# The gate of a two-layer image kernel: paired row strips, two engines that copy the turned magnitudes, a median step on VectorE alone, and attention maxima turned one product earlier

## What is computed

```
layer 0, for each image and channel:
    x = x + relu(-median(x))
    y = relu(up-sample x by 2 with a 7-tap filter); x = down-sample y by 2 with it
layer 1, for each image:
    spec = rfft2(x)
    gate = sigmoid(w2 . gelu(w1 . |spec|))          over the channels of each frequency
    xf   = x + irfft2(spec * gate)
    q    = xf . q_w + q_b                           16384 queries, 4 heads of 16
    k, v = from two strided convolutions of xf (256 and 64 places), layer norm, projection
    out  = softmax(q . k) . v, projected, plus x
```

## Time and profile before

| | us |
|---|---|
| runs | 11229.0, 11243.0, 11243.7 |
| median | 11243.0 |
| the profiled execution | 11240.2 |
| its span, first to last instruction | 11238.7 |
| busy in it: TensorE | 10118.1 (90%) |
| VectorE | 8624.4 (77%) |
| ScalarE | 7246.8 (64%) |
| GpSimd | 5892.8 (52%) |

### The profile page before, as it was taken

One profiled execution on the slowest core, in us unless ns is written; L12 is line 12 of the kernel. 1 busy time (PEld: TensorE's weight loads), 2 busy tenths in 40 slices (PEclk: granted clock), 3 DMA queues, 4 the chain that ended last, 5 costly groups with the idle time before them and its releaser, 6 DMA issues. The chain is left out here.

```text
span 11238.7 us, 198959 instructions
## 1 busy us (share of the span) xinstructions
PE 10118.1 (90%) x68889; PEld 4971.5 (44%) x69001; DVE 8624.4 (77%) x14560; ACT 7246.8 (64%) x12221; POOL 5892.8 (52%) x10577
## 2 busy tenths in 40 slices
PE   2898998989989899899989989899898998989989
PEld 1534435344353543535345353443534435354353
DVE  7777777877778777778777777777787777777777
ACT  5757566665666656667666676656666666675665
POOL 2374463735537365472744737446373553736547
PEclk9999999999999999999999999999999999999999
DMA  2031231312314032140322303123131331403214
GB/s 67 21 78 47 58 85 32 77 36 64 79 32 88 26 73 70 39 89 35 71 54 49 94 22 78 45 59 84 32 79 34 67 76 32 88 32 70 66 40 102
DMA packets 330611, 664.69 MB, mean 59 GB/s; under 512 B 95624, under 2 KB 241160, under 8 KB 308048
## 3 DMA queue, kind: packets, MB, share of 16 engines
q1 hardware_dynamic: 329552, 651.29, 24.4%
HBM read 232.53 MB, written 71.30 MB: 27 GB/s over the span
## 5 line engine op out<-in xcount | busy, mean ns | idle before, releaser
L1314 ACT ACTIVATE R<-ps 128x512 f32<-128x512 f32 x5120 | 2874.7, 593 | 1432.3 <-PE ps L807 1034.8
L1095 DVE TENSOR_REDUCE R<-ps 128x2 f32<-128x640 f32 x3840 | 3042.7, 819 | 798.0 <-PE ps L786 748.7
L265 ACT ACTIVATE R<-R,st 128x1475 bf16<-128x1475 f32 (+1 forms) x1326 | 2077.1, 1566 | 494.9 <-DVE st L337 470.2
L326 DVE TENSOR_SCALAR_CACHE_REDUCE R<-R,st 128x1255 bf16<-128x1255 f32 (+1 forms) x1326 | 1936.9, 1461 | 18.5
L786 PE MATMUL ps<-KST,R 96*128 96x320 bf16 x7680 | 1699.7, 302 | 33.2 <-DMA R<-R 18.3
L807 PE MATMUL ps<-R,KST 104*128 104x512 bf16 x4096 | 1602.5, 394 | 82.7 <-DMA R<-Wk 25.5
L832 PE MATMUL ps<-R 128*32 128x512 f32 x12288 | 1663.2, 615 | 0.0
L1411 POOL TENSOR_TENSOR R<-R 128x256 f32<-128x256 f32 x1440 | 1059.1, 735 | 115.2
L1415 POOL TENSOR_TENSOR R<-R 128x256 f32<-128x256 f32 x1440 | 1050.2, 729 | 120.0
L786 PEld LDWEIGHTS ps<-KST,R 96*128 96x128 bf16 x7680 | 737.4, 99 | 647.7 <-DVE R L1095 154.8
L807 PEld LDWEIGHTS ps<-R,KST 104*128 104x128 bf16 x4096 | 398.4, 98 | 1247.6 <-ACT R L1314 952.5
(11 more groups left out here) (225 smaller groups left out, 19927.3 us busy)
## 6 DMA issues: line engine op xcount, KB each, us to landing
R<-R SPq DMA_DIRECT2D x3072, 64.0 KB, 2.4
R<-xh_in SPq DMA_DIRECT2D x136, 512.0 KB, 4.5
out_dram<-Z SPq DMA_DIRECT2D x68, 1024.0 KB, 3.9
R<-Wk SPq DMA_DIRECT2D x960, 64.0 KB, 2.0
Wk<-Wk SPq DMA_DIRECT2D x960, 64.0 KB, 2.0
R<-xa_in SPq DMA_DIRECT2D x36, 1024.0 KB, 9.9
R<-xb_in SPq DMA_DIRECT2D x36, 1024.0 KB, 11.7
R<-sr_in SPq DMA_DIRECT2D x32, 1024.0 KB, 5.1
```

Source lines behind the costliest of these rows:

```text
L265: e.activation(junka[:, 0:o2 - o1], xc[:, o1:o2], ACT.Sign, bias=mid, scale=-1.0, accum_out=ca[i]).then_inc(md_ca, 1)
L326: e.tensor_scalar(junk[:, 0:o1 - o0], xc[:, o0:o1], mid, None, ALU.is_le, ALU.add, accum_out=cv[i]).then_inc(md_cv, 1)
L1095: e.tensor_reduce(MX[(4 * u + s4) % 2][:, blk_, h0:h0 + 2], ps[:, 2 + 2 * bq:4 + 2 * bq, 0:320], axis=AX.X, op=ALU.max).then_inc(mx, 1)
L1314: e.activation(PB[:, t % 2, w, :], ps[:, w % 2, :], ACT.Exp).then_inc(ex, 1)
```

## The change

Four things change in the order of one image.

1. `ROOTS`: the second of the two roots (steps 8 to 15) becomes two, steps 8 to 13 one step earlier and steps 14 and 15 at the end.
2. The turned magnitudes: VectorE copies the even groups from bank 5, ScalarE the odd ones from bank 6, each with its own semaphore (`mgt`, `mga`).
3. The gates: the groups go in pairs, the products of the two in turn, from two row strips of `HID` into two banks of four (`GATES`), without unused products. Step 20 of the median (`LONE`) is counted by VectorE over whole thirds less one column, ScalarE counts the one column. VectorE runs the step's three pieces behind its last copy of magnitudes; ScalarE's follow the Sigmoids. The 0.36 share, until now from step 21, is unchanged there, and a constant (`less2`) is set at steps 20 and 21.
4. Attention: TensorE's `lay_max` moves from w = 1 to w = 0 in all tiles but the first. ScalarE's copy stays at w = 1.

```diff
-MIDS = [[a + int((0.46 if k < 21 else 0.36) * (b - a)) for a, b in zip(CUTS, CUTS[1:])] for k in range(STEPS)]
+LONE = 20
+MIDS = [[b - 1 if k == LONE else a + int((0.46 if k < LONE else 0.36) * (b - a)) for a, b in zip(CUTS, CUTS[1:])]
+        for k in range(STEPS)]
...
+GATES = (2, 3, 5, 6)
+ROOTS = {7: 0, 13: 8, 15: 14}
...
-                    e.activation(junka[:, 0:o2 - o1], xc[:, o1:o2], ACT.Sign, bias=mid, scale=-1.0,
+                    e.activation(junka[:, 2047:2048] if k == LONE else junka[:, 0:o2 - o1], xc[:, o1:o2], ACT.Sign, bias=mid, scale=-1.0,
...
+                if k in (LONE, LONE + 1):
+                    e.memset(less2, 0.5 * (FEWER[0] - FEWER[k]))
...
-            e.wait_ge(sqt, 2)
+            e.wait_ge(sqt, 3)
...
                 if grp > 1:
-                    e.wait_ge(mgt, grp - 1)
+                    e.wait_ge((mgt, mga)[k], grp // 2)
...
-                slot(1 if grp in (3, 6) else 0)
+                slot(1 if grp == 3 else 0)
...
-            for grp in range(9):
-                k, np_ = grp % 2, 4 if grp < 8 else 1
-                e.wait_ge(gelu, grp // 4 + 1)
-                if grp > 1:
-                    e.wait_ge(sig, grp - 1)
+            for p in range(5):
+                e.wait_ge(gelu, p // 2 + 1)
+                if p == 0:
+                    e.wait_ge(sq, 16)
+                elif p == 1:
+                    e.wait_ge(mgt, 5)
+                    e.wait_ge(mga, 4)
                 else:
-                    e.wait_ge(sq, 16)
...
-                op.then_inc(g_ps, 1)
-                busy(4, 2)
-
-            slot(1)
+                    e.wait_ge(sig, 2 * p - 2)
+                for i in range(4 if p < 4 else 1):
+                    for grp in (2 * p, 2 * p + 1) if p < 4 else (8,):
+                        r0, o = 32 * (grp % 4), 512 * (grp // 4) + 128 * i
+                        gate = ps[:, GATES[grp % 4], 0:512 if p < 4 else 128].rearrange("p (c k) -> p k c", c=C)
+                        op = e.matmul(
+                            gate[:, 2 * i:2 * i + 2, :],
+                            lhsT=HID[r0:r0 + 32, o:o + 128], rhs=c("w2")[r0:r0 + 32, :], start=True, stop=True)
+                        if i == (3 if p < 4 else 0):
+                            op.then_inc(g_ps, 1)
+
+            slot(2)
...
-                    if w == (1 if t else 4) and t + AHEAD - 1 < NT:
+                    if w == (0 if t else 4) and t + AHEAD - 1 < NT:
                         lay_max(t + AHEAD - 1)
...
-            for grp in range(9):
+            for grp in range(0, 9, 2):
...
-                e.tensor_copy(MAGT[:, 512 * grp:512 * grp + 128 * np_], ps[:, 5 + grp % 2, 0:128 * np_]).then_inc(mgt, 1)
-                slot(1 if grp in (3, 6) else 0)
+                e.tensor_copy(MAGT[:, 512 * grp:512 * grp + 128 * np_], ps[:, 5, 0:128 * np_]).then_inc(mgt, 1)
+            slot(3)
...
-                slot(1 if n < 16 else 0)
+                slot(1 if 0 < n < 16 else 0)
...
-                    if x % 8 == 7:
-                        mg = MAG[:, 0:65, 4 * (x - 7):4 * (x + 1)]
+                    if x in ROOTS:
+                        mg = MAG[:, 0:65, 4 * ROOTS[x]:4 * (x + 1)]
...
-            slot(2)
+            for grp in range(1, 9, 2):
+                e.wait_ge(mt_ps, grp + 1)
+                if grp == 1:
+                    e.wait_ge(xr, 4)
+                e.activation(MAGT[:, 512 * grp:512 * grp + 512], ps[:, 6, :], ACT.Copy).then_inc(mga, 1)
...
+            slot(3)
```

More of the change, by code:

```diff
@@ L30 @@
 CUTS = [HALF * i // NP for i in range(NP + 1)]
-MIDS = [[a + int((0.46 if k < 21 else 0.36) * (b - a)) for a, b in zip(CUTS, CUTS[1:])] for k in range(STEPS)]
+LONE = 20
+MIDS = [[b - 1 if k == LONE else a + int((0.46 if k < LONE else 0.36) * (b - a)) for a, b in zip(CUTS, CUTS[1:])]
+        for k in range(STEPS)]
 FEWER = [2.0 * (RANK - sum(b - m for m, b in zip(ms, CUTS[1:]))) for ms in MIDS]
-WINDOWS = [(1, 2, 5) if k < 21 else (0, 3, 6) for k in range(STEPS)]
+WINDOWS = [(1, 2, 5) if k < LONE else (0, 3, 6) for k in range(STEPS)]
 P = C // 2
@@ L57 @@
     "md_v md_max md_p md_cv md_ca md_r md_fs md_g md_lift md_ends md_raise md_ta md_tb md_got md_mm md_row md_end "
-    "f_ps s1 re_ps im_ps sq im sqi mag sqt mz mt_ps mgt h_ps gelu g_ps sig "
+    "f_ps s1 re_ps im_ps sq im sqi mag sqt mz mt_ps mgt mga h_ps gelu g_ps sig "
     "av inv_ps rr xi_ps xf xt_ps xfd xfa "
@@ L94, in program @@
         xc = R6[:, :]
-        junk = R5[:, 0:1024].bitcast(BF16)
+        junk = R5[:, :].bitcast(BF16)
         junka = R5[:, 1024:2048].bitcast(BF16)
@@ L159, in program @@
          md_v, md_max, md_p, md_cv, md_ca, md_r, md_fs, md_g, md_lift, md_ends, md_raise, md_ta, md_tb, md_got, md_mm, md_row, md_end,
-         f_ps, s1, re_ps, im_ps, sq, im, sqi, mag, sqt, mz, mt_ps, mgt, h_ps, gelu, g_ps, sig,
+         f_ps, s1, re_ps, im_ps, sq, im, sqi, mag, sqt, mz, mt_ps, mgt, mga, h_ps, gelu, g_ps, sig,
          av, inv_ps, rr, xi_ps, xf, xt_ps, xfd, xfa,
@@ L589, in tensor @@
                 busy(4, 1)
-                slot(1 if grp in (3, 6) else 0)
+                slot(1 if grp == 3 else 0)
             for grp in range(9):
                 g4, k, w = grp % 4, (grp // 4) % 2, 512 if grp < 8 else 128
-                e.wait_ge(mgt, grp + 1)
+                e.wait_ge((mgt, mga)[grp % 2], grp // 2 + 1)
                 if grp == 0:
@@ L601, in tensor @@
                     op.then_inc(h_ps, 1)
-            for grp in range(9):
-                k, np_ = grp % 2, 4 if grp < 8 else 1
-                e.wait_ge(gelu, grp // 4 + 1)
-                if grp > 1:
-                    e.wait_ge(sig, grp - 1)
-                else:
-                    e.wait_ge(sq, 16)
-                gate = ps[:, 2 + k, 0:128 * np_].rearrange("p (c k) -> p k c", c=C)
-                for i in range(np_):
-                    op = e.matmul(
-                        gate[:, 2 * i:2 * i + 2, :],
-                        lhsT=HID[32 * (grp % 4):32 * (grp % 4) + 32, 512 * (grp // 4) + 128 * i:512 * (grp // 4) + 128 * i + 128],
-                        rhs=c("w2")[32 * (grp % 4):32 * (grp % 4) + 32, :], start=True, stop=True)
-                op.then_inc(g_ps, 1)
-                busy(4, 2)
-            slot(1)
+            for p in range(5):
[5 more added lines that the diff above has]
+                    e.wait_ge(mga, 4)
+                else:
+                    e.wait_ge(sig, 2 * p - 2)
[9 more added lines that the diff above has]
+            slot(2)
             for n in range(1, 18):
@@ L1224, in scalar @@
                 e.activation(GATE[:, :, 8 * grp:8 * grp + 2 * np_],
-                             ps[:, 2 + grp % 2, 0:128 * np_].rearrange("p (c k) -> p c k", c=C), ACT.Sigmoid).then_inc(sig, 1)
+                             ps[:, GATES[grp % 4], 0:128 * np_].rearrange("p (c k) -> p c k", c=C), ACT.Sigmoid).then_inc(sig, 1)
+            slot(3)
             for n in range(18):
@@ L1548, in first_vector @@
             e.memset(ones[:, :], 1.0)
-            e.memset(less2, 0.5 * (FEWER[0] - FEWER[21]))
             e.memset(less1, 0.25 - 0.5 * FEWER[0])
```

## The result

| | before | changed | forecast |
|---|---|---|---|
| median, us | 11242.1 | 11075.5 | 11065 |
| four runs, us | 11229.0 to 11243.7 | 11065.9 to 11077.2 | 11018 to 11135 |
| profiled span, us | 11238.7 | 11073.5 | |

The account below looks back on a forecast made before the run. TensorE bounds the inverse, a chain the stretch before it. Profiled 11240.2 - 154 (root, copies, gates) + 16 (clock) + 4 (first median) - 44 (attention) = 11062; runs' median 2.7 higher: 11065 us, range 11018 to 11135.

Parts of the forecast that it names:

- What bounds the stretch: Between last forward product and inverse, 29.3 us: a chain across engines sets the time, no single busy engine.
- Part 1, the root: Magnitude root in three: last root covers only 520 columns, gain 1.2 us an image, bounds 0 and 1.3.
- Part 2, the copies: Turned magnitudes copied by two engines, median passes gone from between: 3.5 us an image on top of the root's gain.
- Part 3, pairs and lone step: Gates: paired strips keep Sigmoids back to back; VectorE's step 20 ends 0.5 us later, setting the first gated product.
- rival (a): Gates: row strips don't run together, a pair takes 2.05 us, Sigmoids end 0.8 us behind VectorE: 11078 us; chance 0.08.
- What it costs: the clock: Head of the inverse: TensorE's pause brings 3.4 us at 1.2 GHz, losing 1.0 us an image (0 to 1.7), +16 us.
- Part 4: Attention: maxima transposes moved before the second score, 0.17 us in 14 tiles, 2.7 us an image, 44 in all.
- rival (b): Attention: transposes wait for the maxima; nothing gained to 0.3 us lost in each of 16 tiles, 11109 to 11186; chance 0.12.
- Rival (c): Attention: transposes' move gives its upper bound, six late tiles losing their wait (0.5 us each): 11018 us; chance 0.06.
- Rival (d): Median step 20: wide VectorE passes run two elements a cycle, branch ends 3 us earlier, Sigmoids set the end: 11057; chance 0.04.
- Rival (e): Gates through whole inverse: TensorE stays at 1.2 GHz, 37 us an image more, about 11830 us; chance 0.02.
- Rival (f): Chain: ScalarE, with second root and four copies, comes 1.5 us late somewhere: 11089 us; chance 0.08.

Follow-up runs that it names:

- e5: Changed kernel with two roots in place of three, the second over steps 8 to 15 behind the last Square: 11097.4 us.
- e6: Changed kernel with all nine copies of turned magnitudes on VectorE, banks 5 and 6 in turn: 11087.8 us.
- e4: Changed kernel with a pair's gate products one group after the other instead of in turn between two row strips: 11077.5 us.
- e2: Changed kernel with eight unused TensorE products added behind the last gate group only: 11043.3 us.
- e11: Changed kernel with unused products behind the second (four) and fourth (one) pair of gates, none behind the last gate: 11074.0 us.
- e3: Changed kernel with unused products behind the second pair of gates (four), the fourth pair (one) and the last group (eight): 11040.5 us.
- e9: Kernel before with one edit, the two unused products behind each group of gates removed: 11242.5 us.
- e8: Changed kernel with step 20 counted 85% by VectorE, and unused products behind the second (four) and fourth (one) gate pair and last gate (five): 11020.6 us.

## Why the prediction was right, and where not

- **What bounds the stretch.** Right. It was a chain, and each of its marks came within 0.7 us: root 2.8 us behind the last forward product (2.75 forecast), copies 9.3 (9.05), first Sigmoid 13.2 (13.25), Sigmoids' end 17.9 (18.55), gated product 18.9 (19.05).
- **Part 1, the root: 1.2 us.** Right, e5 shows 1.17.
- **Part 2, the copies: 3.5 us.** Size nearly right (3.3), reason half wrong: e6 shows that the second copying engine is worth 0.14. The four copies in 2.78 us of the earlier trace rows had said so.
- **Part 3, pairs and lone step.** The end was right, VectorE's passes set it, by 1.0 us and not 0.5. The role of the pairs was wrong. I priced them by L496 and gave rival (a), strips that don't pair, +13 us. The strips pair at 0.055 us an instruction, and without pairing the cost is 2 us by the median and none in the chain (e4). I had taken 1.15 us as a group's own time, though it was that only between unused products.
- **What it costs: the clock.** This is the mis-sized term. I put 3.4 us at 1.2 GHz, lost in part: 1.0 us, at most 1.7. Measured: mostly 6.8 us at 1.2 GHz, from the last gate on, 4.1 to 4.9 of them in the inverse (4.3 on average), so 2.0 us in each image, above my own bound, and +32 instead of +16. I had looked for its cause in the one pause behind the gates (2.1 us, forecast 2.4). e2 and e11 show that what TensorE does between the gates and that pause both take part; e4, which has no pause between the gates, shows that the pauses there are not what makes the clock fall. The 0.2 us of the second gated product did not show: at full clock the inverse takes 47.20 us in e3, as before. So this stage is 19 us off, and the others, 7 us better than forecast together, bring the miss down to 12 us in the spans.
- **Part 4.** Size right, 2.7 us. In a plain tile the mechanism is the one forecast, the third maxima product held at 1.73 by VectorE, although the second score came 0.15 us later and not 0.07. I had named it a sign of being wrong if a tile's transposes wait for VectorE. In the late tiles they do (at 0.80 instead of 0.59), but those tiles lost nothing by it, so rival (b) did not come. Rival (c) asked for up to 0.5 us in each late tile: 0.06 to 0.09.
- **Rival (d)** did not come, and I had read its rule too narrowly. The Trainium skill ("VectorE: DVE Perf Modes", What auto-detection actually checks) asks for outermost dimensions that are both even or equal in source and destination. A pass reads as many columns as it writes, so by that rule the width of 2729 would go at double rate as well: all three wide passes, and not two. The trace disagrees for both, 3057 and 3056 ns, which is the 1.048 ns a column of the earlier trace rows carried on. The same section says that firmware enables these modes for each instruction; whether it does so for this counting form, no run here shows.

```profile
L332 DVE TENSOR_SCALAR_CACHE_REDUCE R<-R,st 128x2730 bf16<-128x2730 f32 x34 | 103.9, 3057 | 0.6
L332 DVE TENSOR_SCALAR_CACHE_REDUCE R<-R,st 128x2729 bf16<-128x2729 f32 x17 | 51.9, 3056 | 0.7
```

- **Rival (e)**, half clock from the gates through the inverse, was right in kind and not in extent. In e9 it appears in the kernel before as soon as the unused products go: 10.2 to 13.7 us, and in every image it ends 3.0 to 4.7 us into the inverse, while the inverse's own products run.
- **Rival (f)** did not come: ScalarE's copies and second root are nowhere late.

What stays open: where stretches at 1.2 GHz fall elsewhere. They lie in every image of every kernel here, and attention took 303.1 us in e2, 304.6 in e3 and 305.9 in e4 with identical instructions there. That is up to 45 us of the whole, more than several of the edits. The traces say what goes with it: an image's attention stage has 8.6 us at 1.2 GHz in e2, 12.0 in e3 and 13.9 in e4, and over all images of the eleven kernels with this order of attention the stage is 0.38 us longer for each us at half clock in it (correlation 0.92). What decides how much falls there is not known, and no experiment steered it. A comparison of medians by 10 to 20 us is therefore read with the stages beside it.

## What to carry to other kernels

Before an unused product on TensorE is removed, ask which stage behind it is bound by TensorE: here they cost 0.5 us in each group and paid it back by the clock, and what won in the end was to take them from where they lengthen the chain and put them where TensorE would wait anyway (e3, e8). A time read between two neighbours is a time with these neighbours; when they go, ask what may overlap then. And where two branches end within a microsecond of each other, a cut of the later one is worth only the distance to the other, less what the next stage gives back.

## What the runs showed of the hardware

- Instructions of 32 rows by 128 columns start 0.11 us apart in one row strip (e4) and 0.055 apart on average in two strips in turn (32 in 1.72 us, the changed kernel), and neighbouring groups in two strips overlap by themselves when nothing stands between (e4).
- TensorE's clock fell to 1.2 GHz at the end of a gate stage with pauses of 1.21 and 0.26 us (the changed kernel), and just so at the end of one without a pause over 0.16 us (e4, busy 7.95 of the 8.22 us before the fall). In both it was down for 6.8 us, over a pause of 2.1 to 2.3 us. In e9 it was down for 13.65 us in image 8 while TensorE was busy 12.41 of them by the profile.
- Unused products that begin at half clock cost nearly double, 3.51 us for eight (e2) instead of 1.90 (e3), so here they help in full only if they keep the clock from falling.
